# Second mixture: the activation's rounded high half written by ScalarE, in place of a copy on VectorE

## The reference

```python
combine = jnp.sum(jax.nn.one_hot(topi, E, dtype=probs.dtype) * topw[..., None], axis=-2)
h1 = jnp.einsum('bsd,edf->ebsf', mla_out, w1) + b1[:, None, None, :]
h1 = jax.nn.gelu(h1, approximate=False)
h2 = jnp.einsum('ebsf,efd->ebsd', h1, w2) + b2[:, None, None, :]
moe_out = jnp.einsum('bse,ebsd->bsd', combine, h2)
return hs + 0.3 * moe_out
```

## Time and profile before

| | |
|---|---|
| median of 3 runs | 4377.33 us (4373.64 to 4392.21) |
| the profiled execution's own time | 4372.85 us |
| its span | 4371.1 us |
| TensorE, VectorE, ScalarE busy | 93%, 67%, 47% |
| granted TensorE clock, mean | 0.969 of full |
| second mixture: eight stretches | 884.00 us, TensorE busy 876.56 us |

### The profile page before, as it was taken

How to read it: one execution, slowest core, us unless ns; L and a number is a source line. 1 busy time by engine, 2 the same in 40 slices (tenths; PEclk the granted TensorE clock), 3 DMA queues, 4 the chain that set the end, 5 groups by cost and what they waited for, 6 DMA issues and landing times. The chain is left out here.

```text
span 4371.1 us, 73615 instructions
## 1 busy us (share of the span) xinstructions
PE 4059.3 (93%) x28256; PEld 3149.9 (72%) x28256; DVE 2943.5 (67%) x7812; ACT 2055.2 (47%) x3424; POOL 91.6 (2%) x180
## 2 busy tenths in 40 slices
PE   7898998989989899998999989999999999989989
PEld 5675966759768596676966769667696676966768
DVE  7667686676766767666775777657676576775755
ACT  4534555443653535535355353553535535355342
POOL 0000000000000000000000000000000000000000
PEclk8998999989999999999999999999999999999999
DMA  2010610103101030010300103001030011200112
GB/s 101 1 47 11 214 48 1 47 30 126 40 8 49 20 136 30 15 42 30 126 30 15 42 30 126 30 15 42 30 126 30 15 42 49 107 30 15 32 68 92
DMA packets 51767, 228.04 MB, mean 52 GB/s; under 512 B 4832, under 2 KB 21216, under 8 KB 31584
## 3 DMA queue, kind: packets, MB, share of 16 engines
q1 hardware_dynamic: 51424, 223.33, 14.2%
HBM read 202.34 MB, written 20.97 MB: 51 GB/s over the span
## 5 line engine op out<-in xcount | busy, mean ns | idle before, releaser
L1220 DVE TENSOR_REDUCE mx<-w 128x4 f32<-128x1024 f32 x512 | 602.1, 1221 | 144.4 <-PE w L629 134.0
L894 ACT ACTIVATE oth<-w,res 128x256 f32<-128x256 f32 x656 | 277.6, 471 | 588.7 <-PE w L801 476.6
L580 PE MATMUL w<-xnT,stream 128*128 128x256 f32 x1792 | 413.2, 382 | 0.8 <-ACT xnT L886 0.7
L580 PEld LDWEIGHTS w<-xnT,stream 128*128 128x128 f32 x1792 | 338.2, 191 | 49.4 <-ACT xnT L886 1.1
L801 PE MATMUL w<-qodd,va_hi 128*128 128x256 f32 x2048 | 348.5, 284 | 1.3 <-DMA va_hi<-split 0.6
L951 ACT ACTIVATE pt_spread<-w 128x1024 f32<-128x1024 f32 x256 | 257.4, 1029 | 118.6 <-PE w L643 113.8
L801 PEld LDWEIGHTS w<-qodd,va_hi 128*128 128x128 f32 x2048 | 286.8, 189 | 8.8 <-issue 4.3
L1189 DVE SCALAR_TENSOR_TENSOR x<-w,gate,x 128x256 f32<-128x256 f32 x512 | 223.4, 478 | 98.4 <-PE w L810 65.3
L1479 DVE TENSOR_REDUCE mx<-w 128x2 f32<-128x1024 f32 x128 | 155.8, 1226 | 190.6 <-PE w L676 189.8
L629 PE MATMUL w<-ksp,qsp 32*128 32x256 f32 (+1 forms) x2048 | 223.0, 339 | 48.6 <-DVE mx L1220 25.8
L643 PE MATMUL w<-qsp,ksp 32*128 32x256 f32 (+1 forms) x2048 | 219.5, 329 | 45.3 <-DVE qsp L1239 20.4
(11 more groups left out here) (268 smaller groups left out, 8350.6 us busy)
## 6 DMA issues: line engine op xcount, KB each, us to landing
stream_lo<-split SPq DMA_DIRECT2D x56, 1024.0 KB, 4.8
va_hi<-split SPq DMA_DIRECT2D x56, 1024.0 KB, 6.9
stream<-in_moe_dram SPq DMA_DIRECT2D x80, 384.0 KB, 3.1
stream<-in_resident_dram SPq DMA_DIRECT2D x8, 2048.0 KB, 7.7
raw<-in_moe_dram SPq DMA_DIRECT2D x8, 1024.0 KB, 6.6
split<-va_hi SPq DMA_DIRECT2D x8, 1024.0 KB, 8.9
split<-stream_lo SPq DMA_DIRECT2D x8, 1024.0 KB, 10.9
stream<-in_resident_dram SPq DMA_DIRECT2D x8, 1024.0 KB, 4.7
```

Source lines behind the costliest of these rows:

```text
L580: mm = pe.matmul(w[:, col0 + j * T:col0 + j * T + T], weight[:, k, (m0 + j) * P:(m0 + j + 1) * P], act[:, k, :], start=(k == 0), stop=(k = ...
L894: h = act.activation(dst[:, c, :], w[:, c * T:(c + 1) * T], func, bias=bias[:, c:c + 1], **more)
L1220: dve.tensor_reduce(mx[s][:, :, 2 * v:2 * v + 2].rearrange("p t a -> p a t"), w[:, :].rearrange("p (a t k) -> p a t k", a=2, t=TT), AX_X, ...
```

## The change

At each half of an expert ScalarE computes the same two Gelus twice from the same PSUM chunks. It writes them first into `ob_hi`, which has the rounded type, and then into `oth`. VectorE no longer copies, and only subtracts. The semaphores and what they count stay as they are; the first pair waits for what the only pair waited for before. TensorE's order is the same row for row.

```diff
                     w, b = bank_of(step, s, u), W_["f2_b1"][:, 4 * u:4 * u + 4]
+                    biased(ob_hi[s], w, b, 2, ACT.Gelu)
                     biased(oth[s], w, b, 2, ACT.Gelu).then_inc(S["s_gelu2h"], 1)
                     full(act, step, s, u)
+                    biased(ob_hi[s][:, 2:4, :], w[:, 2 * T:], b[:, 2:4], 2, ACT.Gelu)
                     biased(oth[s][:, 2:4, :], w[:, 2 * T:], b[:, 2:4], 2, ACT.Gelu).then_inc(S["s_gelu2"], 1)
...
                     for c, ready in ((0, "s_gelu2h"), (2, "s_gelu2")):
                         dve.wait_ge(*after(ready, "f2.up", s, u))
-                        link(dve.tensor_copy(ob_hi[s][:, c:c + 2, :], oth[s][:, c:c + 2, :]))
                         h = dve.tensor_tensor(oth_lo[s][:, c:c + 2, :], oth[s][:, c:c + 2, :], ob_hi[s][:, c:c + 2, :].bitcast(F32), ALU.subtract)
                     h.then_inc(S["s_up2"], 1)
```

## The result

The changed kernel takes 4399.5 us, the median of 5 runs (4396.1 to 4408.6). Before has 4385.4 in the 5 runs it is compared with; two further runs of before had come in over the 4377.3 known when the prediction was made. The ratio is 1.0036, 95% interval 1.0019 to 1.0053: 0.36% slower, within the 0.5% that was called no change. The time lies in the predicted range, and 19 us over the forecast value: 8 of these are the median of before itself, 11 are the change's (14 us between the medians, 3 forecast).

What follows compares the result with a forecast made beforehand. TensorE was taken to bound the second mixture's stretches, with 7.44 us idle. Terms 1.75 + 1.8 + 1.0 - 1.5 = +3 us on 4372.85, plus 4.5 to the runs' median, gave 4380.5 us; range 4368 to 4404.

Steps and rivals of the forecast that it cites:

- The low half: Second mixture's downs: operand ready 0.31 to 0.40 us later, exposed at five of 10 tight experts; +1.75 us.
- The cover of 0.63 us: Time from the last subtraction to its down's start; the later subtractions were to leave 0.32 or 0.23 us.
- Rival 1: Second mixture's downs: each waits for its own expert's low half; 20 to 45 us slower, priced at 4422 us; chance 0.10.
- rival 1b: Each half's cast and Gelus stand on the path, 0.27 us a half: 69 us on top, 4446 us; chance 0.01.
- The banks: PSUM banks of the ups freed 0.77 to 0.86 us later; five waits, 3.2 less 1.4 us: +1.8 us.
- What stands behind on ScalarE: Instructions after the Gelus (`ctxT`, `ksp`, `qsp`, `xnT`) move back 0.8 us in some 28 experts; +1 us, between 0 and 22.
- VectorE's relief: In 21 experts with late casts VectorE finishes up to 0.92 us earlier; -1.5 us of a possible -7.44.
- the clock: Granted clock in the eight mixture stretches, read as the higher level throughout (1.00, 0.98 in the last); no term for it.
- TensorE's idle was to be about 10 us: Sign: idle in the eight second-mixture stretches about 10 us instead of 7.4, and not over 15.
- L810's waits: Sign: downs' matmul waits for `oth_lo` up from 1.4 to about 3 us; growth beyond some 10 means wrong.
- The waits for ScalarE's `oth`: Sign: matmuls' waits for ScalarE's `oth` or `ob_hi` in the mixture stretches come to 2 to 3 us.
- A Gelu of clearly more than 473 ns: Sign of error: one Gelu into the rounded tile, expected at about 470 ns, takes clearly longer than 473.

Runs made afterwards that it cites:

- the addition alone: Against the kernel before: the Gelus doubled on ScalarE and VectorE's cast kept; ratio 1.0054, +26.8 +- 1.7 us at equal clock.
- The removal alone: Against the kernel before: no cast and no added Gelu, TensorE taking one tile for all three products; ratio 0.9996, -3.5 +- 1.4 us at equal clock.
- the stalls made on purpose: Against the kernel before: two extra passes of Gelus in each half of expert 3, overwritten by the cast; ratio 1.0053, +29.3 +- 1.9 us at equal clock.

## Why the prediction was right or wrong

Right were the range, the verdict of no change at 0.5%, and the frame: TensorE fills these stretches, so 109 us taken off VectorE are worth almost nothing. Term by term:

1. *The low half, +1.75 us.* Small, as forecast, and smaller still: the downs take 0.5 us more from start to start, and the listed waits of L810 for it fell from 1.4 to 0.9. The cover of 0.63 us with 0.23 to 0.32 left did hold, and the addition alone, which overruns it, shows what it was worth (13 us in the downs, 11 without their low clock). Rival 1, by which this wait becomes the loss, and rival 1b are wrong.
2. *The banks, +1.8 us.* Idle for ScalarE's bank release rose from 0.5 to 3.3 us. The forecast was 3.2, less 1.4 for two places where a down idles 0.69 us just behind. Both places are in the trace: there the wait for the bank rose by 0.8 each, and the low half, which had been waited for 0.69 each, is waited for 0.23 at one and not at all at the other, where `ksp` now holds the down for 0.6. So the 3.2 were close to the 2.8 measured, and the offset is what makes the waits of term 1 fall. Together, terms 1 and 2 were put at 3.55 us, and the waits show 2.3.
3. *What stands behind on ScalarE, +1 us.* This is the term that was mis-sized: 1 us was forecast, and 6 us of idle time were measured. The prediction put it between 0 and 22 us and took a value near the low end, with the reason that other work covers it. `kvT` went from 2.5 to 6.2 us of TensorE's idle time, `xnT` from 14.2 to 15.9, `ksp` from 0 to 0.6: +6 us. The prediction counted 28 places and named `xnT`, but not the copy of the router's gate at the first expert. In the trace of before, 30 experts have an instruction of ScalarE within 0.06 us behind their last Gelu, and in 7 of them it is `kvT`, more often than any other. The list of instructions in the section on the change has `kvT` directly behind the first Gelus. TensorE's matmuls at L788 wait for exactly this copy. Nor is its delay 0.8 us: where the Gelus queue behind the table load, it is 1.2 us (pass 3, above), and it is added whole.
4. *VectorE's relief, -1.5 us.* The removal alone gives -3.5 +- 1.4, so it was undersized. In the changed kernel the cast is worth more, since it no longer adds its 0.46 us to each chain: 12 us between the addition alone and the changed kernel.
5. *Not in the sum: the clock.* The prediction read 1.00 in the earlier trace rows and took it as given. In the first profile after, 17.1 us more of the stretches ran at the low clock, 8.5 us; in the second, 3.4 us more. At equal mean clock 14.7 us stay, of which the idle time is 9.7. For most of the other 5 there is an estimate. With half of their low clock taken off, the stretches are 11.5 and 12.1 us longer than before in the two profiles, so some 2 us are short waits inside them that show as no idle time. And 0.001 of mean clock is 8.8 us of low clock (twice 0.001 of the run), for which the line takes off 2.7 us, while in these full stretches it costs 4.4; for the 10 us more of low clock there in the mean of the two profiles that leaves another 2 us. The last microsecond is within the error.

The prediction's own tests: TensorE's idle was to be about 10 us and not over 15, and it is 16.5; L810's waits were to rise to 3 us, and they fell to 0.9. The waits for ScalarE's `oth`, at 2 to 3 us, came out as 3.3. A Gelu of clearly more than 473 ns was to be a sign of being wrong; the mean is 499, and yet it is no sign of a dearer one, since 16 in a row still follow one another every 0.365 us (last section). The 187 us more on ScalarE came out as 169 busy in the stretches, and VectorE's 109 less as 107 in all. That the forecast lay 11 us too low for the change and still in the range is due to the width of the range, which had uncovered `xnT` and `ksp` waits in it.

The Trainium skill's rule for back-to-back activations ("ScalarE: Activation LUTs", section What ACT_TABLE_LOAD costs: an overlap of about 93 ns) is near what the first of a run show here, 0.11 us. Further on in a run the recorded overlap grows: between the pairs recorded at 2088.27 and 2088.99 it is 0.14 us.

## What to carry to other kernels

When an engine that is off the critical path gets more work, don't only price the chain you have lengthened: list every instruction queued behind the added ones on that engine, and look for small copies whose reader on the full engine has nothing else to do. They can pass the delay on whole. In a stretch where TensorE is 99% busy, a stall of a microsecond or more costs its own length and can be followed by several microseconds at half clock; whether the run as a whole pays for these was not shown here. When such a change loses, try it with the first and the last unit of a loop in the old form, since most of its cost may lie there. Here that took the loss from 14.7 to 3.4 us at equal clock, which is still a loss.

## What the runs showed of the hardware that was not expected

- Queued activations are recorded as longer than the time they add. The mean of one Gelu is 499 to 504 ns in the changed kernel against 471 before. In a run of 16, from 478.9 us on, the recorded time grows from 474 to 554 ns, while the ends stay 0.365 us apart (0.73 for a pair), the rate of the earlier trace rows:

```profile
L894 ACT ACTIVATE oth<-w,res 128x256 f32<-128x256 f32 x656 | 286.7, 504 | 116.0 <-PE w L580 115.4
```

- The mean granted clock of one and the same kernel varies from run to run (before: 0.962 to 0.973), and nearly all of the spread of its times goes with it: 2.7 us for 0.001, with 2.3 us left over.
- A stall of TensorE inside a full stretch was often followed by a phase at 1.2 GHz that began within 2 us of TensorE's new start. In the profile of the stalls made on purpose, this was so for six of seven stalls of 1.6 us and more, without a lower mean clock of the whole run.
